# Gated-delta attention on one core: a new beginning, reordered copies, fillers, and each second chunk's heads projected one stretch later

## What is computed

```python
mixed = hidden_states @ W_qkv.T                  # then a causal convolution of 4 taps, and silu
z = (hidden_states @ W_z.T).reshape(b, s, NVH, DV)
beta = jax.nn.sigmoid(hidden_states @ W_b.T)
g = -jnp.exp(A_log) * jax.nn.softplus(a + dt_bias)
...
def step(Sst, inp):
    q_t, k_t, v_t, g_t, b_t = inp
    Sst = Sst * jnp.exp(g_t)[..., None, None]
    kv = jnp.einsum('bhkv,bhk->bhv', Sst, k_t)
    delta = (v_t - kv) * b_t[..., None]
    Sst = Sst + k_t[..., None] * delta[..., None, :]
    o = jnp.einsum('bhkv,bhk->bhv', Sst, q_t)
    return (Sst, o)
...
h_ = o * jax.nn.silu(z)
var = jnp.mean(h_ * h_, axis=-1, keepdims=True)
h_ = h_ * jax.lax.rsqrt(var + EPS) * norm_weight
return h_.reshape(b, s, VAL_DIM) @ W_out.T
...
x = x + _L0_attn_ref(_layernorm(x, axis=-1), ...)
x = x + _L0_ffn_ref(_layernorm(x, axis=-1), ...)   # 8 experts, 2 of them per token, and a shared one
x = x + _L1_attn_ref(_layernorm(x, axis=-1), ...)  # causal attention of 16 heads with rotation, and an MLP
x = x + _L1_ffn_ref(_layernorm(x, axis=-1), ...)   # 8 experts of 512 and a shared one
```

## Time and profile before

| what | value |
|---|---|
| median of 3 runs | 1489.09 us (1488.6 to 1491.01) |
| profiled execution, its own time | 1490.14 us |
| its span | 1488.1 us |
| busy: PE, DVE, ACT, POOL | 86%, 61%, 47%, 21% |
| mean granted TensorE clock | 0.930 of full speed |

### The profile page before, as it was taken

The page is one execution under the profiler, slowest core; times in us unless marked ns, Lnnn a source line. Parts: engine busy times, 40 slices in busy tenths (PEclk is TensorE's granted clock), DMA queues, the critical chain, the costliest instruction groups (busy, mean ns, idle before and its releaser), DMA issues.

```text
span 1488.1 us, 27342 instructions
## 1 busy us (share of the span) xinstructions
PE 1280.1 (86%) x11232; PEld 905.1 (61%) x11272; DVE 911.1 (61%) x2349; ACT 701.7 (47%) x1353; POOL 313.7 (21%) x234
## 2 busy tenths in 40 slices
PE   2678989898988989887986859998998989989898
PEld 2355757566665757566665536765657656666566
DVE  4898889889898988877246233542446433463321
ACT  1647365564847556473441424334452344523442
POOL 5122252516234262515120010000100000000100
PEclk9869999898998989898998779999999999999999
DMA  4000000000000000010400000000000000000000
GB/s 127 4 2 5 1 2 12 2 12 2 12 2 1 12 2 8 2 33 9 151 10 8 2 1 0 8 1 2 8 0 8 1 2 8 0 1 1 2 7 8
DMA packets 15068, 17.72 MB, mean 12 GB/s; under 512 B 2567, under 2 KB 13216, under 8 KB 14560
## 3 DMA queue, kind: packets, MB, share of 16 engines
q1 hardware_dynamic: 12768, 14.09, 2.9%
q0 software_dynamic: 576, 1.76, 0.4%
q10 hardware_dynamic: 1600, 0.12, 0.1%
HBM read 13.87 MB, written 2.10 MB: 11 GB/s over the span
## 4 chain that ended last, share of the span: by engine, by line
PE 53%; DVE 28%; ACT 11%; issue 4%; POOL 2%; DMA 1%; SPq 0%; DVEq 0%; ACTq 0%
PE ps L1577 8%; PE ps L1567 8%; PE ps L1365 6%; DVE arena L1918 5%; DVE arena L1921 4%; PE ps L1124 3%; PE ps L1205 2%; ACT arena L1003 2%; DVE arena L2190 2%; PE ps L1273 2%; PE ps L1669 2%; PE ps L1633 2%; ACT arena L680 2%; ACT arena L704 2%; PE ps L1109 1%
## 5 line engine op out<-in xcount | busy, mean ns | idle before, releaser
L1835 DVE SCALAR_TENSOR_TENSOR arena<-ps,conv_w,arena 128x255 f32<-128x255 f32 (+2 forms) x384 | 163.4, 475 | 17.0 <-ACT arena L671 12.4
L965 ACT ACTIVATE arena<-ps 128x512 f32<-128x512 f32 x144 | 85.2, 597 | 180.7 <-PE ps L1567 180.6
L537 POOL TENSOR_TENSOR rstd<-var_eps,half_power 128x2 f32<-128x2 f32 (+1 forms) x28 | 23.3, 832 | 609.1 <-DVE var_eps L1806 609.0
L1577 PEld LDWEIGHTS ps<-arena 128*128 128x128 f32 x1152 | 132.6, 192 | 24.8 <-issue 9.9
L1577 PE MATMUL ps<-arena 128*128 128x128 f32 x1152 | 136.9, 277 | 7.1 <-ACT arena L965 4.1
L1567 PE MATMUL ps<-arena 128*128 128x512 f32 x288 | 134.3, 612 | 0.0
L2161 DVE SCALAR_TENSOR_TENSOR arena<-ps,gates,arena 128x128 f32<-128x128 f32 x128 | 36.0, 344 | 113.8 <-PE ps L1577 113.5
L531 POOL TENSOR_SCALAR arena<-arena 32x1024 f32<-32x1024 f32 x32 | 88.4, 2764 | 53.4 <-DVE arena L1930 51.4
L1918 DVE TENSOR_TENSOR arena<-arena 128x30 f32<-128x30 f32 (+14 forms) x240 | 95.2, 397 | 7.3
L2227 DVE TENSOR_REDUCE arena<-ps 128x8 f32<-128x2048 f32 (+1 forms) x24 | 54.8, 2292 | 63.2 <-PE ps L1633 63.2
L1921 DVE TENSOR_TENSOR arena<-arena 128x30 f32<-128x30 f32 (+14 forms) x240 | 83.8, 349 | 8.2
(11 more groups left out here) (248 smaller groups left out, 2849.4 us busy)
## 6 DMA issues: line engine op xcount, KB each, us to landing
arena<-in_routed_up SPq DMA_DIRECT2D x1, 2048.0 KB, 9.5
arena<-in_routed_down SPq DMA_DIRECT2D x1, 2048.0 KB, 15.3
x_ln<-in_x SPq DMA_DIRECT2D x8, 128.0 KB, 2.3
arena<-in_w_mix SPq DMA_DIRECT2D x1, 1024.0 KB, 11.0
x_in<-in_x SPq DMA_DIRECT2D x8, 128.0 KB, 2.4
out_x<-x_res SPq DMA_DIRECT2D x8, 128.0 KB, 1.9
arena<-out_x SPq DMA_DIRECT2D x4, 256.0 KB, 2.8
out_x<-arena SPq DMA_DIRECT2D x4, 256.0 KB, 2.2
```

Of the source, the lines that this page charges most:

```text
L965: act.activation(hid1[half][:, i, :], ps[:, banks[i], :], ACT.Gelu).then_inc(s["mgelu"], 1)
L1577: mm = pe.matmul(ps[:, bank, c * P:(c + 1) * P], hid1[half][:, i, c * P:(c + 1) * P], m_down[:, e, i, :], start=(i == 0), stop=(i == HT1 - 1))
L1835: ins = dve.scalar_tensor_tensor(conv_tile(f, m)[:, sh:SEQ], ps[:, PAIR_BANK[p], j * SEQ:(j + 1) * SEQ - sh], conv_w[:, m, TAPS - 1 - sh:T ...
```

## The change

1. **The beginning.** The loads of SP have a semaphore each, x first; each user waits for its own. POOL's large clears, the scaling of `w_out` and the whole of the expert weights move behind the masked decays of iteration −2. ACT loads the table of Exp with a function of a dummy tile (`act_pad`, scale 0), and takes the exponential of `A_log` behind that of sequence 0's exponents. DVE norms sequence 0 first.
2. **Copies.** On ACT `second_block(n)` stands ahead of `solved32(n, ·)`, and `solve64(·, 0)` waits for the first of the three copies of `merged32` only (`tt32_ready`).
3. **Fillers.** In `pair_layers(0)` PE runs 20, 20 and 14 fillers where the later pairs have late experts.
4. **Heads.** `turn_heads(i - 1, 1, ·)`, their copies, `project_out(i - 1, n, 1, ·)` and `residual(i - 1, 1)` move from the product stretch to the end of the inversion stretch, ahead of those of `(i, 0)`; both chunks are turned through bank 6 now (7 for the last sequence's chunk 1), and projected into 6 and 7.

```diff
-            sp.dma_start(w_ba[:, :], t["w_ba"]).then_inc(s["w_a_in"], 16)
...
+            sp.dma_start(w_ba[:, :], t["w_ba"]).then_inc(s["w_ba_in"], 16)
+            sp.dma_start(w_mix, t["w_mix"]).then_inc(s["w_mix_in"], 16)
...
@@ gpsimd
-            pool.wait_ge(s["w_a_in"], 64)
-            pool.wait_ge(s["small_in"], 16 * 6)
-            pool.tensor_scalar(w_out[:, :, :], w_out[:, :, :], norm_w[:, 0:1], None, ALU.mult)\
-                .then_inc(s["norm_scaled"], 1)
...
-                    after(pool, "y_psum", CH * i)
+                    after(pool, "y_psum", CH * i - 1)
...
+                if it == -2:
+                    cleared_tiles()
+                    scaled_w_out()
+                    weights_of_experts()
@@ scalar
-            act.wait_ge(s["small_in"], 16 * 6)
-
-            act.wait_ge(s["alog_split"], 2)
-            act.activation(exp_a[:, :, :], exp_a[:, :, :], ACT.Exp).then_inc(s["setup_act"], 1)
-
-            act.wait_ge(s["setup_pool"], 3)
+            act.wait_ge(s["setup_pool"], 1)
+
+            act.wait_ge(s["act_step"], 1)
+            act.activation(act_pad[:, :], act_pad[:, :], ACT.Exp, scale=0.0).then_inc(s["act_step"], 1)
...
-                act.activation(tt[32:64, hs, 0:32], src[32:64], ACT.Copy)
+                act.activation(tt[32:64, hs, 0:32], src[32:64], ACT.Copy).then_inc(s["tt32_ready"], 1)
...
-                if has_i and i > 0:
-                    turned_heads(i - 1, 1, 0)
                 if has_f:
                     exponentials(f)
...
                     seed(f, 4)
+                if has_i and i > 0:
+                    turned_heads(i - 1, 1, 0)
+                    turned_heads(i - 1, 1, 1)
                 if has_i:
                     turned_heads(i, 0, 0)
...
+                    second_block(n)
                     solved32(n, 0)
                     solved32(n, 1)
-                    second_block(n)
@@ tensor
             pe.wait_ge(s["consts_in"], 16)
-            pe.wait_ge(s["setup_pool"], 3)
-            pe.wait_ge(s["setup_dve"], 2)
-            pe.wait_ge(s["w_a_in"], 64)
-            pe.wait_ge(s["norm_scaled"], 1)
...
-                pe.wait_ge(s["u32_ready"], 2 * n + 1)
+                pe.wait_ge(s["tt32_ready"], 2 * n + 1)
+                if g == 1:
+
+                    pe.wait_ge(s["u32_ready"], 2 * n + 1)
...
-                if c == 1 and has_n:
-                    pe.wait_ge(s["u64_ready"], 4 * (i + 2))
-                if c == 1:
-                    pe.wait_ge(s["hz_ready"], 4 * i + 3)
+                if i == 0 and c == 0:
+                    pe.wait_ge(s["norm_scaled"], 1)
+                if c == 1 and i + 1 < SEQS:
+
+                    pe.wait_ge(s["hz_ready"], 4 * (i + 1) + 3)
...
                 if has_f:
                     project(f, 4, n, has_n)
+                if has_i and i > 0:
+                    turn_heads(i - 1, 1, 0)
+                    turn_heads(i - 1, 1, 1)
+                    project_out(i - 1, n, 1, has_n)
...
+                else:
+                    pe.wait_ge(s["merged"], it * G + 2)
+                    keep_busy(0, 20)
                 turn_tokens(1, h_tok, 4)
...
+                else:
+                    keep_busy(1, 20)
                 turn_tokens(2, h_tok, 5)
...
+                else:
+                    keep_busy(0, 14)
@@ vector
-            dve.wait_ge(s["setup_pool"], 3)
...
+                if it == -2:
+                    constants_of_masks()
+                    split_a_log()
...
-                if has_i and i > 0:
-                    residual(i - 1, 1)
                 if has_n:
                     steps_of_inverse(lanes, n, 0, 9)
...
                     steps_of_inverse(lanes, n, 22, 27)
+                if has_i and i > 0:
+                    residual(i - 1, 1)
                 if has_i:
                     sum_squares(me, i, 1)
```

More of the change, by code:

```diff
@@ L364, in prod_of, with ht_bank @@
             return (k // 2) % 2 if p > 0 else 0
+        def ht_bank(i, c):
+            return 7 if c == 1 and i == SEQS - 1 else 6
         def over_heads(ap, n):
@@ L939, in _ @@
             hidden_tiles_of(0, 13)
-            tables = [1]
+            tables = [2]
             def pair_layers(it, more):
@@ L1090, in gate @@
                     pe.wait_ge(s["hz_ready"], 4 * i + 3 + j)
+                    if j == 0:
+                        after(pe, "x_updated", CH * i)
                 pe.matmul(ps[:, (7, 5)[j], :], hT3[:, n % 3, c * P:(c + 1) * P], w_z[:, 512 * j:512 * (j + 1)],
@@ L1266, in outputs @@
                 pe.wait_ge(s["e_ready"], 4 * i + 2 * c + g + 1)
-                if c == 0 and g == 0:
-                    after(pe, "x_updated", CH * i)
                 if c == 1 and g == 0:
@@ L1376, in _ @@
                     beta_decay(f)
-                if has_i and i > 0:
-                    turn_heads(i - 1, 1, 0)
                 if has_n:
@@ L1381, in _ @@
                     key_products(n, 3)
-                if has_i and i > 0:
-                    turn_heads(i - 1, 1, 1)
                 if it == SEQS - 1:
@@ L1394, in _ @@
                     key_products(n, 7)
-                if has_i and i > 0:
-                    project_out(i - 1, n, 1, has_n)
                 if has_f:
```

118 lines of the change are left out of this document (71 added, 47 removed).

## The result

The changed kernel took 1505.22 us (median of 5 runs, 1499.75 to 1509.79); the kernel before, beside it, 1490.55 (5 runs, 1488.6 to 1491.23). The ratio is 1.0103, 95% interval 1.0076 to 1.013: **slower by 1.0%**, where 1473 us had been forecast. The profiled execution has a span of 1507.7 us at a mean granted clock of 0.918, 19.6 us more than the span before.

The account below looks back on a forecast made before the run. No engine bounds the kernel everywhere; PE holds 53% of the chain that ended last. Beginning −13.0, heads +3.0 and fillers −5.5 sum to −15.5 from the profiled 1490.14 us, forecasting 1473 after adjusting to the median, range 1460 to 1484.

Parts of the forecast that it names:

- the clock falls with the filler work gone: Rival, inversion stretches: 3.0 us lost each; in half of six, 1482 us, chance 0.24; in all, 1491, chance 0.04.
- iteration 0 also lacks other work in front: Argument against a clock fall, though iteration 0's inversion stretch ran at clock 0.87 and took 39.77 us against 36.76.
- The beginning: Start of the kernel: the first exponents on DVE come earlier with waits and clears removed, −13.0 us (8.1 to 13.6).
- Product stretch: Iterations 1 to 6: without the moved heads it takes iteration 0's 17.37 us for 18.18, −0.81 each.
- End of the inversion stretch: Moved turns and projection there make DVE's transposed inverse 0.9 us later and PE ready 1.8 us later.
- the +3 in the sum: Moved heads over six iterations: between +0.1 and +1.0 us each, taken as +0.5.
- Copies: Solve stretch: reordered ACT copies shorten PE's chain by at most 6 us over eight times; taken as 0.
- Fillers: PE's three holes in pair layer 0: fillers hold the clock behind them, 0, −2.0 and −3.5, sum −5.5 us.
- The rival that the clock holds in the solve stretch: With PE's idle ahead of the solve gone, the wait for seeds goes, −1.8 us an iteration: 1459.5 us, chance 0.15.
- The rival on the other side: End of inversion: gates and fillers at half clock make PE 7.6 us late for the solve: 1511 us, chance 0.04.

Follow-up runs that it names:

- beginning_alone: The kernel before with only the new beginning (part 1 of the change): 1479.47 us, ratio 0.9919.
- all_holes_filled: The kernel before with new beginning, pair layer 0 fillers, moved heads, 9 or 14 fillers in iterations 0 to 6's holes, fewer ahead of the solve: 1476.26 us.
- heads_alone: The kernel before with only the moved heads (part 4 of the change): 1518.62 us, ratio 1.0199.
- first_hole_filled: The kernel before with the new beginning, pair layer 0's fillers and nine fillers behind project(f, 0) in iteration 0 alone: 1470.87 us, ratio 0.9871.
- first_copy_only: The kernel before with the new beginning, pair layer 0's fillers and the solve's wait for only the first of three copies: 1480.73 us, ratio 0.9924.
- no_heads: The changed kernel with the moved heads put back in the product stretch; beginning, copies and fillers as changed: 1480.72 us, ratio 0.9931.
- beginning_fillers: The kernel before with only the new beginning and pair layer 0's fillers (parts 1 and 3): 1474.84 us, ratio 0.9904.
- middle_filled: The changed kernel with three and three fillers in the middle of the product stretch and none at its end: 1512.7 us, ratio 1.0156.

## Why the prediction was wrong

**The step that failed** is the sum's silence on the clock in the inversion stretch. The terms took PE's and DVE's work there at clock 1.00 and put "the clock falls with the filler work gone" among the rivals, at 3.0 us an iteration in half of the iterations and a chance of 0.28. The mechanism of that rival was the right one for the larger part: the stretches lost +2.4 to +6.8 us an iteration, 28.3 together, of which 0.8 each are the residual and the later sum of squares, and the clock fell behind the emptied product stretch in five of the six. In iteration 1 it did not; there, and again in 2, 3 and 6, it fell at the turns at the end of the inversion stretch, and no rival had a price for that: the last one even held that PE has no hole up to there, where it waits 0.98 and 1.06 us. The argument that held the chance down, "iteration 0 also lacks other work in front", did not carry: nine fillers in that one place brought iteration 0 from 39.57 us at clock 0.91 to 36.68 at 1.00, though it lacked the rest as before. The earlier trace rows had shown the case exactly, a product stretch without an earlier sequence's heads and the fallen clock behind it, and I took the first half of it as a gain (−0.81) and not the second as its price.

**Why it was sized too low.** Iteration 0's 3.0 us is what the fall costs with the old work at the stretch's end. After the move the stretch lost that much or less in iterations 1, 4 and 5 (2.4 to 3.6) and more in 2, 3 and 6 (5.2 to 6.8). The trace shows why: a fall behind the hole lasted 6.8 us in iterations 2, 4 and 5 and cost 2.8, and lasted 10.2 in 3 and 6; one of 3.4 us at the turns cost 1.6 more in 1, 2 and 3. That these come from PE's waits between the turns is argued from their place and from the kernels that don't have them, not tested by filling them. The rule of the Trainium skill that was weighed ("TensorE: Matmul & The Clock Gate", Part 1) has activity release the throttle. The runs agree in direction: with 2.18 us of idle ahead of the solve the time was 1505 us, with nine fillers in it 1483.

**Term by term.**
- The beginning: forecast −13.0 (8.1 to 13.6), measured −12.5 at the exponents and −12.0 in beginning_alone. Right. The table `a_b` was in at 12.45 for 16.70, so it was the bound, 0.8 us later than ACT's. It landed 9.0 us after its issue for 13.2 before (8.2 in beginning_alone), with the expert weights' load moved away; SP's loads were reordered too, so which of the two did it is not shown. The rule of the Trainium skill that was weighed ("DMA: Bandwidth & Descriptors", Queues, rings and completion order) points the same way. POOL's moved work stayed hidden: the first inversion began 12.7 us sooner.
- Product stretch: forecast −0.81 for each of six, measured 17.37 us for 18.18 in iteration 1, and 5.0 us over the six. Right to the last digit, and it was this gain that opened the hole.
- End of the inversion stretch: forecast +0.9 on DVE, measured 37.54 for 36.76, +0.8, where the clock held; PE's lateness of 1.0 us behind it as forecast. So with the clock held the moved heads are worth −0.8 + 0.8 = 0, the lower end of what was worked out (+0.1 an iteration), and not the +3 in the sum; all_holes_filled found nothing better.
- Copies: forecast 0 (down to −6): no gain, a cost of up to 6 not excluded.
- Fillers: forecast −5.5, of it 0, −2.0 and −3.5; measured 0, −2.5 and −2.5 in the profile, and 2 to 5 less in the time. Right in size, the split between the second and the third off by 1.
- The rival that the clock holds in the solve stretch: PE's idle ahead of the solve was gone, and that stretch's mean clock in iterations 1 to 5 rose from 0.75 to between 0.76 and 0.87 in the kernels with moved heads, but it was no shorter. That PE's work isn't what sets its length is argued from this. The rival was wrong in its gain.
- The rival on the other side had PE late by the gates at half clock. The kernel was slower, but not by that: PE was late by 1.0 us where the clock held.

**The sum.** −12.5 − 5.0 + 28.3 − 5.0 makes +5.8, and the solve stretches 5.3 more. Of the rest, up to the 19.6 of the profiled spans, 6.5 us lie in pair layer 2, which no edit touched. Windows from the first turn of tokens of pair 2 to its second, before and after:

```profile
1143.58:1225.28 81.70, 72.67 (x679) 48.14 (x681) 32.77 (x66) 33.47 (x62) 3.51 (x3) 0.98 0.00 1
```

```profile
1155.49:1243.68 88.19, 79.21 (x680) 52.73 (x681) 32.76 (x66) 34.03 (x62) 3.51 (x3) 0.90 0.01 1
```

The same code took 81.7 us at clock 0.98 and 88.2 at 0.90. In the other profiled executions this stretch of pairs 1, 2 and 3 took between 81.7 and 88.2 us without a rule that I could find; heads_alone, with the old beginning, lost nothing there, first_hole_filled, with the new one, neither. Differences of up to 6.5 us in one execution are of the size by which the runs of one kernel scatter (first_copy_only 1473.3 to 1481.7), and so no_heads and first_copy_only can't be told from beginning_fillers. What sets it is open.

## What to carry to other kernels

Where an iteration runs at full clock, the work that fills its idle places is part of what keeps it there: before work is moved out of a stretch, read in the trace how long PE will then wait directly ahead of its next long run of products, and put a filler of that length in the same place. Look at the place that the work moves to as well: turns and projections that wait for other engines brought idles of 1 us with them there, and the clock fell among them. If one iteration of a pipeline already lacks the work in question, compare its whole course with the others', clock included, and take every difference as the forecast. Here the change was worth making without its second and fourth parts, and with nine more fillers in iteration 0: 1470.9 us for 1490.8.

## What the runs showed of the hardware

- Behind an idle of PE of 2.18 us directly ahead of a run of products the granted clock fell to half in 25 of 29 stretches; in the changed kernel and middle_filled the first 32 products behind it then took 4.64 to 7.01 us, for the 3.76 that they took in iteration 1 of the changed kernel, where it did not fall.
- In the changed kernel's iterations 1 to 6 the falls lasted 3.4 to 10.2 us each; the mean clock of the inversion stretch was 0.81 to 0.96, and the stretch took 39.2 to 43.6 us for 36.8.
- An idle of 1.32 us with less work ahead of it was followed by a fall in 5 of 5 stretches, one of 1.39 to 1.47 us with 2.1 us of work directly ahead of it in 0 of 10.
- 1.3 us more of PE work in the middle of the stretch did not help, and nine fillers (2 us) in the hole gave 22 us back.
- Untouched code in the pair layers ran at clock 0.98 in one execution and 0.90 in another, 81.7 and 88.2 us.
